# Attention over rows: one ScalarE operation copies all transposed probabilities; bias, relu and second expansion moved in the order of work

## The chip, the core and the metric

The program runs on one core of one Trainium2 chip. The time is that of the device for one execution of the whole program, in microseconds (us). Five engines have queues of their own, each worked off in order: TensorE (PE), VectorE (DVE), ScalarE (ACT), GpSimd (POOL) and SyncE (SP); semaphores tie them together.

## The reference

Eight batches of 128 tokens of width 256 pass through four pairs of attention and feed-forward. The second pair is the one that the change touches:

```python
x = x + _L1_xattn_ref(_layernorm(x), ctx, ...)   # 16 heads of 16; q, k rms-normalised over 256
x = x + _L1_ffn_ref(_layernorm(x), ...)          # 4-bit fake quantisation, 256 -> 1024 -> 256
# _L1_xattn_ref
q = rms_norm(x @ Wq + bq, gq); k_img = rms_norm(ctx_img @ Wk_img + bk_img, gk_img)
v_img = ctx_img @ Wv_img + bv_img
out = _attend(q, k_img, v_img) @ Wo + bo         # the text half is zero: the context is short
# _L1_ffn_ref
h = x_q @ W1_q.T + b1_q;  h_q = fake_quant(relu(h), s2, 0, 15)
out = h_q @ W2_q.T + b2_q
```

## The kernel before

The program works through stages 0 to 8 in one block; stages 2 and 3 (this pair) run together in `s23_pe`, `s23_act`, `s23_dve` and `s23_pool`, and their last feed-forward steps are woven into stage 4 (`s47_pe` and its fellows). The order of work on each engine is written out by hand in a loop over windows w from -4 to 15, with k = w // 2: two windows, even and odd, for each batch k. A half h = 2n + c is one group of eight heads of batch n. In window w TensorE does

- `scores(w+1)` (L1376) and `turn_probs(w)` (L1383: transposes of eight heads' probabilities into two banks of PSUM, the same two that held the scores);
- in an even window `output(k-1)` (L1406, projection of the attention), `down(k-3)` (L1442, second product of the feed-forward), then the projections of batch k+2 (L1340, L1346);
- in an odd window `turn_rows(k)` (L1419) and `turn(k+2)` (L1361, transposes of normalised queries and keys);
- `up(k-2, 0 or 1)` (L1434, first product of the feed-forward, in halves of 512 columns) and `weigh(w)` (L1398, probabilities by values, with row sums).

VectorE does `maxima(w+1)` (L1590) and its half of the copies of the transposed probabilities, `copy_probs(w)` (L1597, the second bank, 128x512). In an even window follow `add(k-1)` and `feed(k-3)` (residuals with the moments of the layernorm; L1620, L1637, L1640), `apply` (L134, the layernorm itself), `bias(k+2)` (L1564) and `values(k+2)` (L1571). In an odd window it does `normalise(k+2)` (L1581) ahead of the copy, `divide(w-1)` (L1603, L1607), and after the copy `quantise(k-2, 0)`, `divide(w)`, `quantise(k-2, 1)` (L1626, L1630).

ScalarE copies the first bank (L1485), takes the exponentials (`exps`, L1493), in an even window the sums of squares of batch k+2 (`squares`, L1504, which wait for `bias`) and then `relu(k-2, 0)` (L1527); in an odd window `copy_rows` (L1518), `copy_qk` (L1512) and `relu(k-2, 1)`. GpSimd turns the sums into inverse roots (L1686, L1689; for the layernorms L139), adds the output bias (L1702), builds the diagonal of keys (L1696) after `copy_qk`, and quantises the rows for `up` (L1706 to L1712). `c_PT` and `c_PTv` count the two copies, `c_o` counts finished `divide`s, `c_x` finished `add`s.

Who waits for what: `weigh(w)` for both copies; `divide(w)` for `weigh(w)`; `turn` for `normalise`, which waits for the roots of the squares; `up(n, 0)` for the first operation of `feed(n-1)` (they share a bank); `up(n, 1)` for `relu(n, 0)`; `quantise(n, i)` for `relu(n, i)`; `down(n)` for `quantise(n, 1)`.

Of the kernel before, what the change touches and what calls it, by code (L numbers as in the profile page):

```python
# [26 lines left out]
ACT = mybir.ActivationFunctionType  # L27
AX = mybir.AxisListType

B, T, D = 8, 128, 256  # L30
# [41 lines left out]
def build(nc, x, ctx, ctxT, mask, maskT, kvmask, a_wqT, a_wkT, a_wvT, a_bq, a_bk, a_bv, a_sel,  # L72
# [5 lines left out]
    with ex:  # L78
# [6 lines left out]
        P = ex.enter_context(nc.psum_tensor("P", [128, 8, 512], F32))  # L85
# [1144 lines left out]
        HALVES = 2 * B  # L1230
# [100 lines left out]
        def s23_pe(pe):  # L1331
# [32 lines left out]
            def scores(h):  # L1364
                n, c = divmod(h, 2)
                pe.wait_ge(c_qkT, n + 1)
                pe.wait_ge(c_kbd, h + 1)
                if h == 1:
                    pe.wait_ge(c_qkT, 2)
                    pe.wait_ge(c_v, 2)  # L1370
                if h >= 2:
                    pe.wait_ge(c_PT, h - 1)
                    pe.wait_ge(c_PTv, h - 1)
                for i in range(2):
                    half = slice(64 * i, 64 * i + 64)
                    t = pe.matmul(P[:, 2 + 2 * c + i, :], c_qT[n % 2][half, c, :], c_kb[n % 2][half, c], start=True,  # L1376
                                  stop=True)
                t.then_inc(c_s, 1)
# [8 lines left out]
            def weigh(h):  # L1387
                n, c = divmod(h, 2)
                pe.wait_ge(c_PT, h + 1)
                pe.wait_ge(c_PTv, h + 1)  # L1390
                pe.wait_ge(c_v, n + 1)
                if c == 0 and n > 0:
                    pe.wait_ge(c_x, n)
                for what in range(2):
                    for i in range(2):
                        for r in range(4):
                            j = 2 * r + i
                            t = pe.matmul(P[32 * r:32 * r + 32, 6, c * D + what * T:c * D + what * T + T],  # L1398
                                          c_one[:, i, :] if what else c_vp[n % 3][:, 8 * c + j, :],
                                          c_pt[h % 2][:, j, :], start=(i == 0), stop=(i == 1))  # L1400
                t.then_inc(c_pv, 1)
# [47 lines left out]
            for w in WINDOWS:  # L1449
                k, odd = divmod(w, 2)  # L1450
                if 0 <= w + 1 < HALVES:
                    scores(w + 1)
                if 0 <= w < HALVES:
                    turn_probs(w)
                if not odd:
                    if 0 <= k - 1 < B:
                        output(k - 1)
                    if 0 <= k - 3 < B:
                        down(k - 3)
                    if 2 <= k + 2 < B:  # L1460
                        project_context(k + 2)
                        project_rows(k + 2)
                    elif k == -2:
                        project_rows(0)
                else:
                    if 0 <= k - 1 < B:
                        turn_rows(k, 1)
                    if 0 <= k + 2 < B:
                        turn(k + 2)
                    if k == -2:  # L1470
                        project_rows(1)
                if 0 <= k - 2 < B:
                    up(k - 2, odd)
                if 0 <= w < HALVES:
                    weigh(w)
                if 1 <= w + 5 < B:
                    turn_routed(w + 5)
            return output, turn_rows, up, down

        def s23_act(act):  # L1480
            def copy_probs(h):
                act.wait_ge(c_t, h + 1)
                if h >= 2:
                    act.wait_ge(c_pv, h - 1)
                act.activation(c_pt[h % 2][:, 0:4, :].rearrange("p j t -> p (j t)"), P[:, 2 + 2 * (h % 2), :],  # L1485
                               ACT.Copy).then_inc(c_PT, 1)

            def exps(h):
                act.wait_ge(c_mx, h + 1)
# [17 lines left out]
            def copy_qk(n):  # L1507
                act.wait_ge(c_tr, n + 1)
                if n >= 2:
                    act.wait_ge(c_s, 2 * n - 2)  # L1510
                    act.wait_ge(c_kbd, 2 * n - 2)
                act.activation(c_qT[n % 2].rearrange("p j t -> p (j t)"), P[:, QK_BANK[n], :], ACT.Copy).then_inc(c_qkT, 1)  # L1512
# [25 lines left out]
            for w in WINDOWS:  # L1538
                k, odd = divmod(w, 2)
                if 0 <= w < HALVES:  # L1540
                    copy_probs(w)
                if 0 <= w + 1 < HALVES:
                    exps(w + 1)
                if not odd:
                    if 0 <= k + 2 < B:
                        squares(k + 2)
                else:
                    if 0 <= k - 1 < B:
                        copy_rows(k, 1)
                    if 0 <= k + 2 < B:  # L1550
                        copy_qk(k + 2)
                if 0 <= k - 2 < B:
                    relu(k - 2, odd)
                if 1 <= w + 5 < B:
                    copy_routed(w + 5)
            return copy_rows, relu

        def s23_dve(dve):
# [26 lines left out]
            def maxima(h):  # L1585
                dve.wait_ge(c_s, h + 1)
                if h >= 2:
# [1 line left out]
                bank = 2 + 2 * (h % 2)  # L1589
                dve.tensor_reduce(c_m[h % 2], P[:, bank:bank + 2, :].rearrange("p a (j t) -> p (a j) t", t=T), AX.X,  # L1590
                                  ALU.max, negate=True).then_inc(c_mx, 1)

            def copy_probs(h):
                dve.wait_ge(c_t, h + 1)
                if h >= 2:
                    dve.wait_ge(c_pv, h - 1)
                dve.tensor_copy(c_pt[h % 2][:, 4:8, :].rearrange("p j t -> p (j t)"),  # L1597
                                P[:, 3 + 2 * (h % 2), :]).then_inc(c_PTv, 1)

            def divide(h):  # L1600
                n, c = divmod(h, 2)
# [46 lines left out]
            for w in WINDOWS:  # L1648
                k, odd = divmod(w, 2)
                if 0 <= w + 1 < HALVES:  # L1650
                    maxima(w + 1)
                if odd and 0 <= k + 2 < B:
                    normalise(k + 2)
                if odd and 0 <= w - 1 < HALVES:
                    divide(w - 1)
                if 0 <= w < HALVES:
                    copy_probs(w)
                if not odd:
                    if 0 <= k - 1 < B:
                        add(k - 1)  # L1660
                    if 0 <= k - 3 < B:
                        feed(k - 3)
                    if 0 <= k - 1 < B:
                        apply("attend", k - 1)
                    if 0 <= k - 3 < B:
                        apply("feed", k - 3)
                    if 0 <= k + 2 < B:
                        bias(k + 2)
                        values(k + 2)
                else:  # L1670
                    if 0 <= k - 2 < B:
                        quantise(k - 2, 0)
                    if 0 <= w < HALVES:
                        divide(w)
                    if 0 <= k - 2 < B:
                        quantise(k - 2, 1)
                if 2 <= w + 6 < B:
                    routed_row(dve, w + 6)
# [1474 lines left out]
```

## Time and profile before

| | |
|---|---|
| median of 3 runs | 1213.58 us (1206.4 to 1214.52) |
| profiled execution | 1215.49 us, span 1213.5 us |
| mean granted TensorE clock | 0.947 of full |
| stages 2 and 3 with `weigh` | about 437 to 563 us of the span |

A span is the time from the first to the last instruction; the time of a run has some 2 us around it. Positions below are microseconds from the start of the span.

### The profile page before, as it was taken

To read this page: it belongs to the slowest core of one execution; us is meant where nothing else is said; L and a number is where in the kernel's file an instruction comes from. 1 tells how busy PE (TensorE), PEld (TensorE's weight loads), DVE (VectorE), ACT (ScalarE), POOL (GpSimd) and SP (SyncE) were. 2 spreads that over 40 slices of the span, in tenths; PEclk is the share of its full clock that TensorE was granted. 3 is DMA by queue.
4 is the path that set the end of the run, shared out by engine and by line. 5 is a ranking of instruction groups with operands and counts; after the bars stand their busy time and mean duration, and the time that the engine had idled before them with its cause. 6 is when DMAs were issued, how large, how long until landed. Compare 5 with 4: busy or idle time off the path is not lost.

```text
span 1213.5 us, 20040 instructions
## 1 busy us (share of the span) xinstructions
PE 1058.6 (87%) x6826; PEld 803.0 (66%) x6826; DVE 717.7 (59%) x1700; ACT 502.6 (41%) x1785; POOL 319.9 (26%) x440
## 2 busy tenths in 40 slices
PE   6898788699999868878999999999789999996694
PEld 3665555489999745656878777776556666664472
DVE  5576775711222276887656565566677777775544
ACT  2255557233333144665433334243445555554120
POOL 6252331112332233553100000001212222220572
PEclk9899999689999968989999999999999999999797
DMA  6764442689888406100111101122000000000795
GB/s 194 268 209 143 142 133 81 240 314 331 317 329 321 141 26 227 52 1 31 36 55 36 36 1 36 35 88 88 1 1 5 5 5 6 6 5 13 223 312 180
DMA packets 85218, 141.72 MB, mean 117 GB/s; under 512 B 10090, under 2 KB 58490, under 8 KB 79202
## 3 DMA queue, kind: packets, MB, share of 16 engines
q1 hardware_dynamic: 71193, 116.84, 29.1%
q0 software_dynamic: 4416, 12.06, 2.9%
q10 hardware_dynamic: 9508, 11.55, 2.8%
q8 instruction: 55, 0.90, 0.3%
q14 instruction: 46, 0.37, 0.1%
HBM read 117.51 MB, written 22.72 MB: 116 GB/s over the span
## 4 chain that ended last, share of the span: by engine, by line
PE 60%; DVE 12%; DMA 9%; issue 7%; ACT 4%; SPq 4%; POOL 3%; DVEq 0%; POOLq 0%; ACTq 0%
PE P L968 6%; PE P L978 6%; PE P L1928 4%; PE P L1968 4%; PE P L2114 4%; PE P L2061 4%; DMA scr_qk<-big 3%; PE P L1919 3%; PE P L2880 2%; PE P L2067 2%; PE P L2103 2%; PE P L2089 2%; DMA big<-placed 2%; PE P L2897 1%; PE P L1940 1%
## 5 line engine op out<-in xcount | busy, mean ns | idle before, releaser
L139 POOL TENSOR_TENSOR lrs<-lve,mhalf 128x1 f32<-128x1 f32 x64 | 36.6, 572 | 328.3 <-DVE lve L130 284.2
L576 DVE TENSOR_REDUCE small<-P 128x2 f32<-128x512 f32 x128 | 84.2, 683 | 44.4 <-PE P L403 44.4
L1009 ACT ACTIVATE big<-P,big 128x128 f32<-128x128 f32 x184 | 52.4, 368 | 124.5 <-PE P L968 124.5
L2255 ACT ACTIVATE big<-P,small 128x128 f32<-128x128 f32 x128 | 45.2, 366 | 128.4 <-DVE small L2438 128.4
L656 ACT ACTIVATE big<-P 128x512 f32<-128x512 f32 x128 | 73.6, 599 | 59.0 <-PE P L423 52.0
L968 PE MATMUL P<-big 128*128 128x128 f32 x736 | 87.5, 278 | 0.6 <-DMA big<-b_w 0.5
L968 PEld LDWEIGHTS P<-big 128*128 128x128 f32 x736 | 85.6, 195 | 1.1 <-DMA big<-b_w 1.1
L1111 DVE COPY big<-P 128x256 f32<-128x256 f32 x23 | 9.8, 425 | 125.9 <-PE P L978 125.9
L978 PE MATMUL P<-big 128*128 128x256 f32 x368 | 83.1, 379 | 0.0
L271 PE MATMUL P<-CT,big 128*128 128x256 f32 (+1 forms) x224 | 69.7, 441 | 5.7 <-ACT big L248 4.4
L978 PEld LDWEIGHTS P<-big 128*128 128x128 f32 x368 | 68.2, 190 | 8.4
L403 PE MATMUL P<-big 90*128 90x256 bf16 x256 | 51.1, 282 | 13.8 <-DVE small L576 12.2
L1919 PE MATMUL P<-XNT,big 128*128 128x128 f32 x512 | 62.6, 275 | 0.0
L2114 PE MATMUL P<-big 128*128 128x256 f32 x256 | 61.8, 385 | 0.4 <-DVE big L2635 0.4
L2356 ACT ACTIVATE big<-P 128x512 f32<-128x512 f32 x32 | 19.1, 597 | 102.5 <-PE P L2067 102.5
L2061 PE MATMUL P<-big,XNT 128*128 128x512 f32 x128 | 60.4, 594 | 1.1 <-DVE big L2579 1.1
L1968 PE MATMUL P<-big 128*128 128x256 f32 x256 | 60.6, 380 | 0.0
L1928 PE MATMUL P<-big,CT 128*128 128x512 f32 x128 | 60.1, 592 | 0.0
L1919 PEld LDWEIGHTS P<-XNT,big 128*128 128x128 f32 x512 | 59.7, 192 | 0.2 <-issue 0.2
L2347 ACT ACTIVATE big<-P,small 128x128 f32<-128x128 f32 x128 | 56.7, 459 | 5.2 <-DVE small L2624 5.2
L2429 DVE COPY big<-P 128x512 f32<-128x512 f32 x32 | 22.1, 691 | 60.5 <-PE P L1928 60.4
L1152 POOL DMA_INDIRECT moe_y<-big x23 | 25.0, 1089 | 122.3 <-DVE big L1111 122.3
(387 smaller groups left out, 2530.8 us busy)
## 6 DMA issues: line engine op xcount, KB each, us to landing
big<-b_w SPq DMA_DIRECT2D x23, 1028.0 KB
big<-b_w SPq DMA_DIRECT2D x23, 1024.0 KB
big<-scr_qk SPq DMA_DIRECT2D x96, 96.0 KB
big<-keys_t SPq DMA_DIRECT2D x8, 1024.0 KB, 6.4
big<-i_wgu SPq DMA_DIRECT2D x23, 352.0 KB
keys_t<-XNT ACTq DMA_DIRECT2D x24, 256.0 KB, 2.1
big<-moe_y SPq DMA_DIRECT2D x16, 256.0 KB, 4.3
big<-i_wd SPq DMA_DIRECT2D x23, 176.0 KB
```

What stands on the lines that cost most here:

```text
L271: t = pe.matmul(P[:, key_bank(p), lo:hi], k_wts[:, g, k, 128 * j:128 * j + 128], CT[:, k, 512 * r + lo:512 * r + hi], start=(k == 0), stop ...
L576: dve.tensor_reduce(negM[:, h, :], P[:, h % 2, :].rearrange("p (c s) -> p c s", c=2), AX.X, ALU.max, negate=True).then_inc(a_max, 1)
L656: act.activation(ER[:, g % 8], P[:, second_bank(i), :].rearrange("p (c t) -> p c t", c=2), ACT.Exp).then_inc(a_e, 1)
L968: m = pe.matmul(P[:, 2 * (j % 2) + f // 4, f % 4 * 128:f % 4 * 128 + 128], w1x[j % 3][:, k * F0 + f * 128:k * F0 + f * 128 + 128], xgT[j % ...
L978: m = pe.matmul(P[:, 6 + j % 2, 0:D], hT[j % 2][:, f, :], w2x[j % 3][:, f, :], start=(f == 0), stop=(f == FC - 1))
L1009: act.activation(hT[j % 2][:, f, :], P[:, 2 * (j % 2) + f // 4, f % 4 * 128:f % 4 * 128 + 128], ACT.Gelu_apprx_tanh, bias=w1x[j % 3][:, 2 ...
L1919: t = pe.matmul(P[:, 0, j * T:j * T + T], e_wqs[:, g, k, j * 128:j * 128 + 128], XNT[:, k, b * T:b * T + T], start=(k == 0), stop=(k == KD ...
L1928: t = pe.matmul(P[:, 2, :], CT[:, k, b * T:b * T + T], e_wvs[:, g, k, :], start=(k == 0), stop=(k == KD - 1))
L1968: t = pe.matmul(P[:, 7, 0:D], e_o[:, j, :], e_wos[:, 4 * g + j, :], start=(g == 0 and j == 0), stop=(g == 3 and j == 3))
L2061: t = pe.matmul(P[:, 0, :], XNT[:, k, b * T:b * T + T], h_wqs[:, g, k, :], start=(k == 0), stop=(k == KD - 1))
L2114: t = pe.matmul(P[:, 7, 0:D], h_o[:, j, :], h_wos[:, 4 * g + j, :], start=(g == 0 and j == 0), stop=(g == 3 and j == 3))
L2347: t = act.activation(h_pr[m % 2][:, j, :], P[:, 4 - 2 * (m % 2), j * T:j * T + T], ACT.Exp, bias=h_bi[m % 2][:, j:j + 1], scale=h_rq[:, m ...
```

## The change

In `s23` alone. ScalarE copies both banks in one operation of 128x1024 and VectorE's copy goes, with its semaphore; `weigh(h)` gets a wait for `divide(h-1)` in its place. Three steps change their place in a queue: on TensorE `up(k-2, 1)` goes ahead of `turn(k+2)`; on ScalarE `relu(k-2, 0)` goes ahead of `squares(k+2)`, and `copy_qk` ahead of `copy_rows`; on VectorE `bias(k+2)` goes ahead of both `apply`.

```diff
@@ scores, weigh (PE)
                 if h >= 2:
                     pe.wait_ge(c_PT, h - 1)
-                    pe.wait_ge(c_PTv, h - 1)
...
                 pe.wait_ge(c_PT, h + 1)
-                pe.wait_ge(c_PTv, h + 1)
+                if h > 0:
+                    pe.wait_ge(c_o, h)
@@ order of PE, odd window
                         turn_rows(k, 1)
+                    if 0 <= k - 2 < B:
+                        up(k - 2, 1)
                     if 0 <= k + 2 < B:
                         turn(k + 2)
...
-                if 0 <= k - 2 < B:
-                    up(k - 2, odd)
+                if not odd and 0 <= k - 2 < B:
+                    up(k - 2, 0)
@@ copy_probs (ACT)
-                act.activation(c_pt[h % 2][:, 0:4, :].rearrange("p j t -> p (j t)"), P[:, 2 + 2 * (h % 2), :],
-                               ACT.Copy).then_inc(c_PT, 1)
+                bank = 2 + 2 * (h % 2)
+                act.activation(c_pt[h % 2].rearrange("p j t -> p (j t)"),
+                               P[:, bank:bank + 2, :].rearrange("p a n -> p (a n)"), ACT.Copy).then_inc(c_PT, 1)
@@ order of ACT
                 if not odd:
+                    if 0 <= k - 2 < B:
+                        relu(k - 2, 0)
                     if 0 <= k + 2 < B:
                         squares(k + 2)
                 else:
+                    if 0 <= k + 2 < B:
+                        copy_qk(k + 2)
                     if 0 <= k - 1 < B:
                         copy_rows(k, 1)
-                    if 0 <= k + 2 < B:
-                        copy_qk(k + 2)
-                if 0 <= k - 2 < B:
-                    relu(k - 2, odd)
+                    if 0 <= k - 2 < B:
+                        relu(k - 2, 1)
@@ order of DVE (the function copy_probs of DVE is removed)
-                if 0 <= w < HALVES:
-                    copy_probs(w)
...
                     if 0 <= k - 3 < B:
                         feed(k - 3)
+                    if 0 <= k + 2 < B:
+                        bias(k + 2)
                     if 0 <= k - 1 < B:
                         apply("attend", k - 1)
                     if 0 <= k - 3 < B:
                         apply("feed", k - 3)
                     if 0 <= k + 2 < B:
-                        bias(k + 2)
                         values(k + 2)
```

## Rows read from the trace of the kernel before

**Rows 1.** The page, busy time of each engine, its share of the span, instructions.

```profile
PE 1058.6 (87%) x6826; PEld 803.0 (66%) x6826; DVE 717.7 (59%) x1700; ACT 502.6 (41%) x1785; POOL 319.9 (26%) x440
```

**Rows 2.** Busy time by stretch: batches 3, 4 and 5, then stage 4.

```profile
489.10:504.40 15.30, 12.60 (x140) 9.55 (x141) 13.52 (x29) 9.99 (x35) 7.98 (x10) 1.00 0.10 26
504.40:519.70 15.30, 12.55 (x136) 9.43 (x136) 13.53 (x29) 9.98 (x35) 7.97 (x10) 0.98 0.01 3
519.70:535.70 16.00, 13.89 (x136) 10.36 (x136) 13.46 (x29) 10.05 (x35) 7.98 (x10) 0.91 0.01 2
...
562.00:640.00 78.00, 75.88 (x545) 63.89 (x545) 48.66 (x119) 30.91 (x116) 9.02 (x12) 1.00 0.16 47
```

Columns: stretch, its length, then busy us and instructions of PE, PEld, DVE, ACT and POOL, the granted clock, the DMA share and GB/s.

**Rows 3.** Timeline of batch 4, from one odd `weigh` to the next.

```profile
504.37 1.08 PE L1398 MATMUL P<-big 128*32 128x128 f32 x32 [0.73 <-issue]
...
504.80 1.62 ACT L1527 ACTIVATE big<-P,small 128x128 f32<-128x128 f32 x4
...
506.71 0.71 DVE L1626 TENSOR_SCALAR big<-big 128x512 f32<-128x512 f32 x1
...
507.24 1.20 POOL L1706 TENSOR_SCALAR big<-XNT,small 128x256 f32<-128x256 f32 x1
...
507.45 0.58 DVE L1630 TENSOR_SCALAR big<-big 128x512 bf16<-128x512 f32 x1
...
509.09 0.67 DVE L1597 COPY big<-P 128x512 f32<-128x512 f32 x1
...
510.84 1.03 PE L1346 MATMUL P<-big,XNT 128*128 128x256 f32 x4
...
511.70 0.61 PE L1434 MATMUL P<-big 128*128 128x128 bf16 x8
...
513.79 0.68 DVE L1564 TENSOR_TENSOR big<-P,big 128x512 f32<-128x512 f32 x1
514.31 0.86 PEld L1383 LDWEIGHTS P<-idf,big 128*128 128x128 f32 x8 [0.76 <-issue]
...
514.51 0.42 ACT L1504 ACTIVATE big<-big 128x256 f32<-128x256 f32 x1 [3.13 <-DVE big L1564]
...
515.32 1.48 ACT L1527 ACTIVATE big<-P,small 128x128 f32<-128x128 f32 x4
...
516.51 1.33 DVE L1581 SCALAR_TENSOR_TENSOR big<-big,small 128x256 f32<-128x256 f32 x2 [0.51 <-POOL small L1689]
...
517.77 0.94 DVE L1603 RECIPROCAL big<-P 128x128 f32<-128x128 f32 x1
...
517.90 0.66 PE L1361 MATMUL P<-idf,big 128*128 128x128 f32 x4 [2.06 <-DVE big L1581]
...
518.95 0.68 DVE L1597 COPY big<-P 128x512 f32<-128x512 f32 x1
...
519.74 1.94 PE L1398 MATMUL P<-big 128*32 128x128 f32 x32 [0.73 <-issue]
```

Columns: start, length, engine, line, operation, out<-in, count, and in brackets the idle time before it with what ended it.

**Rows 4.** Groups by line, 437 to 562 us, ScalarE.

```profile
L1485 ACT ACTIVATE big<-P 128x512 f32<-128x512 f32 x16 | 9.6, 598 | 25.2 <-PE P L1383 25.2
```

Columns after the bar: busy us, mean ns of one, idle us before them and its end.

**Rows 5.** Timeline of other batches: `weigh` or `up` and their waits.

```profile
458.12 1.93 PE L1398 MATMUL P<-big 128*32 128x128 f32 x32 [1.18 <-issue]
...
474.47 1.68 PE L1398 MATMUL P<-big 128*32 128x128 f32 x32 [1.18 <-issue]
...
484.25 1.48 ACT L1527 ACTIVATE big<-P,small 128x128 f32<-128x128 f32 x4
...
542.88 0.88 PE L1434 MATMUL P<-big 128*128 128x128 bf16 x8 [2.25 <-DVE big L1637]
...
561.91 1.08 PE L1398 MATMUL P<-big 128*32 128x128 f32 x32 [0.71 <-issue]
```

**Rows 6.** Busy time by stretch, two of those at a low clock.

```profile
456.00:465.00 9.00, 7.54 (x53) 5.06 (x54) 6.07 (x12) 2.90 (x10) 2.27 (x4) 0.62 0.01 2
...
519.00:523.00 4.00, 3.27 (x37) 2.02 (x36) 2.63 (x7) 2.78 (x9) 2.44 (x3) 0.57 0.00 0
```

More of the change, by code:

```diff
@@ L1591, in maxima @@
                                   ALU.max, negate=True).then_inc(c_mx, 1)
[L1593 to L1598, printed above, removed]
             def divide(h):
```

## The prediction

> **What bounds the kernel now.** I read the page first, then busy time by stretch, then the timeline of the two stages. The page gives TensorE 87% of the span and VectorE 59% [rows 1]; that says nothing about the stage that changes. By stretch it turns round: in batches 3 and 4 VectorE is busy 13.5 us of 15.3, TensorE 12.6, ScalarE 10.0 [rows 2]; in stage 4 behind them TensorE is busy 75.9 us of 78 [rows 2], so what the two stages save should arrive at the end whole: stage 4 is limited by TensorE's own work and only starts earlier. Its loads are no limit either (DMA share 0.16 there [rows 2]).
>
> The timeline of batch 4 [rows 3] then shows the ring. I take one batch from the start of its predecessor's odd `weigh` to its own: 504.37 to 519.74, 15.37 us. TensorE stands idle twice in it: 2.06 us before `turn` (517.90), which waits for `normalise`, and 0.73 us before `weigh` (519.74). That second wait is put down to issue, but it ends 0.1 us after VectorE's copy (518.95 and 0.68), for which `weigh` also waits. `normalise` (516.51) waited for the roots of the squares; the squares (514.51) had waited 3.13 us for `bias` (513.79); and `bias`, whose data were there at 511.87 (510.84 and 1.03), came last in VectorE's even window, behind its copy (509.09), `add`, `feed` and both `apply`. So VectorE's queue sets the batch: two copies of 0.68 and a badly placed `bias` lie on the ring.
>
> **The change part by part, on batch 4.**
>
> Step 1, the even copy of VectorE (0.68) goes. `add` starts that much earlier, and `feed` ends near 511.95 in place of 512.62 (two steps of 0.4 `apply` lie between it and `bias` at 513.79, with a wait of 0.4 for a root).
>
> Step 2, `bias` forward: it would start at 511.95, just behind its data at 511.87, so 1.8 us earlier. What is late next is not `bias` but ScalarE, because of step 3.
>
> Step 3, `relu(2, 0)` ahead of `squares`: the relu can start when `up` ends (511.70 and 0.61, so 512.35) and takes 1.48 [rows 3]; the squares start at 513.73 (instructions of one queue overlap by 0.1 there), not 514.51. Only 0.8 of the 1.8 us arrives. Between squares and `normalise` lie 2.00 us (514.51 to 516.51), unchanged: `normalise` at 515.73. `maxima` in front of it waits for `scores`, which end at 514.4 as before, and ends at 515.66: just in time.
>
> Step 4, the odd copy (0.68) goes. `normalise` to `divide` is 1.26 (516.51 to 517.77), `divide` itself 1.18 (to 518.95) and 0.1 more to TensorE. The new wait of `weigh` for `divide(w-1)` is what ends last: 515.73 + 1.26 + 1.18 + 0.1 = 518.3, against 519.74. The wait adds nothing of its own: VectorE's copy stood behind that `divide` in the queue, so `weigh` waited for it already. Behind the waiting `weigh` stands only the next `scores`.
>
> Step 5, `up(2, 1)` ahead of `turn`: it fills 0.5 us of the idle time before `turn`, and `turn` then lies 0.5 us closer to `weigh`, with 0.6 us to spare against `divide`. Worth nothing by itself, nor does it cost, as `relu(2, 0)` is done by then (515.1).
>
> Step 6, ScalarE's copy of 1024 columns. The trace shows none. 512 columns take 598 ns [rows 4] and 256 take 420 [rows 3], so 0.70 ns a column and 0.96 us; two operations of 512 would be 1.20. I take 1.0, as it is one operation, and keep 0.95 and 1.2. It can't be below what one bank takes. In the even window it ends long before `weigh`. In the odd one `turn_probs` ends at 515.4 (514.31 and about 1.1), ScalarE has finished the squares at 514.7, and the copy is there at 516.5, 1.8 us before `weigh`. But everything behind it moves: exponentials, `copy_qk`, `copy_rows`, and last `relu(2, 1)`, which began 0.43 us after the start of `weigh` (504.80 against 504.37 a batch earlier) and ended 2.05 after it. It would end about 2.65 after it, and `quantise(k-3, 1)`, which began 2.34 after it (506.71), slips by 0.3; `down` behind it had a margin of 0.2. So a second ring through ScalarE, relu, `quantise`, `down`, projections, `up`, is as long as the first: 0.1 per batch at a copy of 1.0, 0.3 at 1.2. Batch 4 comes to 14.05 us: 1.3 saved.
>
> The Trainium skill speaks against the swap: "ScalarE: Activation LUTs", section Rules for kernel authors, sends cheap elementwise functions to VectorE. Here VectorE's copy of a bank takes 680 ns and ScalarE's 598 [rows 3, 4], and it is VectorE that is full. The same page (What ACT_TABLE_LOAD costs) gives an ACTIVATE with immediate operands as 186 ns and 0.833 ns a column, which would be an estimated 1.04 us for 1024; no row here shows that size, and the sum would be the same within 0.1.
>
> **The other batches.** Batch 3 is like 4 (15.3 us [rows 2]): 1.2. Batches 0 and 1 have no feed-forward and `bias` waits for its data; only the odd copy is on their path, before the `weigh`s at 458.12 and 474.47 [rows 5], each with a wait of 1.18 behind the copy: 0.6 each. Batch 2 has the first `relu(0, 0)`, at 484.25 behind the squares [rows 5]. Put ahead of them it delays the squares by 1.2 us, of which `maxima` hid 0.9; the rest and some slower `normalise` eat up the 0.68 of the odd copy: a loss of 0.1. Batch 5 lasted 16.0, part of it at a low clock; with that left as it was TensorE's own chain to `up` is on the path, and only 0.6 is won. In batch 6 and 7 there are no projections, and `up` waits for `feed` (2.25 us at 542.88 [rows 5]), so both copies count, the even one and the odd one: 1.3 and 1.2 (the last `weigh` is at 561.91 [rows 5]). Sum: 0.6 + 0.6 - 0.1 + 1.2 + 1.3 + 0.6 + 1.3 + 1.2 = 6.7 us.
>
> **The clock.** Four times in these batches TensorE fell from 2.4 to 1.2 GHz: in 456 to 465 (mean 0.62), in 519 to 523 (0.57) [rows 6], and, as the lengths of 1.68 for the `weigh` at 474.47 and 0.88 for the `up` at 542.88 show (1.08 and 0.61 at full clock [rows 3, 5]), there. `weigh` at 519.74 took 1.94 for 1.08. The two idle times before a fall sum to 3.4, 2.05, 2.8 and, as one, 2.25 us; before 504.37 it was 2.66 and nothing fell. After the change the sums should be 2.8 (batch 0), 1.3 (batch 1), 1.4 (batches 3 to 5) and 1.65 (batch 6, one copy less). All but the first are below anything that fell. In their own batches the falls cost an estimated 2.7, 1.6, 1.4 and 1.3 us: half of the stretch at the low clock, where TensorE was on the path. I count the two that are farthest from falling again, 1.6 and 1.4: 3.0 us.
>
> Together 9.7 us. Against its own time that is 1215.49 - 9.7 = 1205.8; against the median of 1213.58, 1.9 lower than the profiled execution, 1203.9. About 1% (12.1 us) is what a measurement of this kernel can tell from no change; its three runs already spread over 8.1 us.
>
> **The rivals.**
>
> A, the clock comes back everywhere: also the falls in batches 0 and 6, 2.7 and 1.3 more, so 13.7 in all: 1199.9. For it: the idle times shrink everywhere. Against: in batch 0 the 2.2 us before its `turn` stay.
>
> B, the clock falls as often as before, elsewhere perhaps: 6.7 us, 1206.9. For it: 2.66 us of idle time did not fell it and 2.05 did, so the idle sums alone don't decide.
>
> C, VectorE's copy was hidden after all, or something as long takes its place: the ring through ScalarE turns out longer than I count. If the copy costs 1.2, and `relu(k-2, 1)` pushes `quantise` by 1 us in batches 3 to 5, these win 0.3 each instead of 1.2: 3 us less, without the clock's share: 1210. A version of it is the lock that the skill describes: `quantise` moves towards GpSimd's L1706, and a VectorE operation held for the whole of that one (1.20) would add 0.6 to 0.9 to each of three batches. In the trace L1630 ran beside L1706 (507.45 beside 507.24 to 508.44) and took 0.58 [rows 3] where its twin takes 0.43: a slowing by 0.15, no hold. The Trainium skill, "SBUF — State Buffer", says that the loser of the shared port pair fully blocks; by this row it doesn't here.
>
> D, slower: the clock falls in places where it now doesn't. TensorE's idle time is split anew, 0.8 before `turn` and 0.6 before `weigh`, in every batch. A fall costs 1.4 us where TensorE's chain is the ring, which it now is. Four more falls, in batches 2, 3, 4 and 7, cost 5.6 and leave 1.1 of 6.7; from the fifth on the kernel is slower, and with three more of 1.4 in stage 4 it would be at 1216.7. Against: less idle time in each batch.
>
> **How the numbers follow.** Forecast (6.7 and about half of the clock's share) 0.42; A 0.22; B 0.18; C 0.13; D 0.05. The forecast alone spans 1202 to 1206. A and its spread reach 1197, C reaches 1211; for 8 in 10 I take 1197 to 1211.5. Faster by over 1% (below 1201.4): most of A and a fifth of the forecast, 0.31. Within 1%: 0.65. Slower by over 1%: 0.04, from D.
>
> **What would show it.** Odd `weigh` to odd `weigh` in batches 3 and 4 at 14.0 to 14.3 us; the copy at 0.95 to 1.05 us; squares 0.7 us earlier, directly behind `relu(k-2, 0)`; `normalise` at once behind `maxima`; TensorE idle for 0.6 to 0.8 us before `turn` and before `weigh`, with `weigh` just behind `divide`; VectorE idle in the even window instead (for `bias`' data and for `scores`). VectorE's busy time lower by 16 times 0.68, 10.9 us; ScalarE's higher by 16 times 0.4, 6.4. From the last `weigh` to the end the same 652 us. I would be wrong if stage 4 gave the gain back, if the copy were far above 1.2, or if the ring of ScalarE's relu were the longer one by more than 0.3.

## The result

The median of nine executions is 1202.14 us (1198.61 to 1208.41), before 1214.14 us over nine (1206.4 to 1217.05, and one slow execution of 1895.58 us that the ratio leaves out). The ratio is 0.991 with an interval of 0.9889 to 0.9931, so the kernel is 10.9 us faster, between 8.4 and 13.5. The profiled execution took 1198.61 us, the fastest of the nine; its span is 1196.8 us, against 1213.5.

Not all of these 16.7 us belong to the change. I cut both spans at the first and the last `weigh` of the stage:

| us | before | after | saved |
|---|---|---|---|
| start to `weigh(0)`, code unchanged | 450.55 | 446.11 | 4.44 |
| `weigh(0)` to `weigh(15)` | 111.36 | 98.58 | 12.78 |
| `weigh(15)` to the end | 651.59 | 652.11 | -0.52 |

The first line is chance between two executions of the same code (in the profiles of the experiments below `weigh(0)` starts anywhere from 444.56 to 451.57). The third says that stage 4 and all behind it only start earlier. The busy time by stretch has the change in it (columns as in [rows 2]): batches 1, 4 and 6, then 78 us of stage 4.

```profile
453.09:466.11 13.02, 11.32 (x114) 7.94 (x115) 10.31 (x21) 7.80 (x25) 5.43 (x8) 1.00 0.52 146
493.41:507.42 14.01, 12.58 (x137) 9.49 (x138) 12.26 (x27) 11.03 (x35) 7.86 (x10) 1.00 0.01 3
521.43:533.21 11.78, 9.49 (x120) 6.79 (x121) 10.32 (x22) 8.79 (x25) 7.05 (x8) 1.00 0.01 1
552.00:630.00 78.00, 75.87 (x520) 64.15 (x519) 46.65 (x117) 32.29 (x123) 6.10 (x9) 1.00 0.17 47
```

A batch of 14.01 us stands where 15.3 stood; VectorE is busy 12.3 in it, not 13.5; the clock is full in all of them, also in batches 1 and 6. The timeline of the changed kernel, batch 4, answers to [rows 3]. Lines of the file have moved by a few: L1569 is `bias`, L1530 relu, L1507 squares, L1595 maxima, L1488 the copy, L1586 normalise, L1601 divide, L1624 and L1628 the two steps of quantise; on GpSimd L1693 is the diagonal of keys (two operations) and L1699 the output bias.

```profile
493.41 1.08 PE L1398 MATMUL P<-big 128*32 128x128 f32 x32 [0.58 <-issue]
...
500.74 0.61 PE L1434 MATMUL P<-big 128*128 128x128 bf16 x8
...
501.10 0.69 DVE L1569 TENSOR_TENSOR big<-P,big 128x512 f32<-128x512 f32 x1
...
501.39 1.51 ACT L1530 ACTIVATE big<-P,small 128x128 f32<-128x128 f32 x4 [0.97 <-PE P L1434]
...
502.77 0.43 ACT L1507 ACTIVATE big<-big 128x256 f32<-128x256 f32 x1
...
503.47 1.23 DVE L1595 TENSOR_REDUCE small<-P 128x8 f32<-128x1024 f32 x1 [0.64 <-PE P L1375]
...
504.48 1.02 ACT L1488 ACTIVATE big<-P 128x1024 f32<-128x1024 f32 x1 [0.79 <-PE P L1382]
...
504.71 0.73 POOL L1699 TENSOR_TENSOR X<-X,big 128x256 f32<-128x256 f32 x1
...
504.78 1.34 DVE L1586 SCALAR_TENSOR_TENSOR big<-big,small 128x256 f32<-128x256 f32 x2
...
506.05 0.94 DVE L1601 RECIPROCAL big<-P 128x128 f32<-128x128 f32 x1
...
506.18 0.66 PE L1361 MATMUL P<-idf,big 128*128 128x128 f32 x4 [0.85 <-DVE big L1586]
...
507.42 1.08 PE L1398 MATMUL P<-big 128*32 128x128 f32 x32 [0.58 <-issue]
...
507.68 0.43 DVE L1628 TENSOR_SCALAR big<-big 128x512 bf16<-128x512 f32 x1
...
508.14 2.04 POOL L1693 TENSOR_TENSOR big<-big,small 128x512 f32<-128x512 f32 x2 [2.69 <-ACT big L1515]
...
508.41 1.60 ACT L1530 ACTIVATE big<-P,small 128x128 f32<-128x128 f32 x4
...
510.04 0.43 DVE L1624 TENSOR_SCALAR big<-big 128x512 f32<-128x512 f32 x1 [0.20 <-ACT big L1530]
```

`relu` starts as soon as `up` is done, the squares right behind it, `normalise` right behind `maxima`, `weigh` 0.1 us after `divide`. The one copy of 1024 columns takes 1.02 us. Two rows of GpSimd matter for what follows: the diagonal starts 0.03 us after the first half's `quantise` has ended (508.11), and `normalise` starts 0.07 us after GpSimd's output bias.

### The profile page after: what moved, and what is told of

It is laid out like the page before. It is cut to its first block, busy times and chain, and to the rows that moved or that the text cites. A ratio compares the mean times of both kernels' runs of the same rounds, so it can differ in the third digit from the quotient of the medians.

```text
span 1196.8 us, 19996 instructions
## 1 busy us (share of the span) xinstructions
PE 1049.0 (88%) x6826; PEld 797.5 (67%) x6826; DVE 709.2 (59%) x1684; ACT 510.2 (43%) x1785; POOL 320.1 (27%) x440
## 4 chain that ended last, share of the span: by engine, by line
PE 62%; DVE 11%; DMA 8%; issue 6%; ACT 5%; SPq 4%; POOL 3%; DVEq 0%; POOLq 0%; ACTq 0%
PE P L968 7%; PE P L978 7%; PE P L1925 4%; PE P L1965 4%; PE P L2111 4%; PE P L2058 4%; DMA scr_qk<-big 3%; PE P L1916 3%; PE P L2064 2%; PE P L2877 2%; PE P L2100 2%; PE P L2086 2%; PE P L1937 2%; SPq L329 2%; DMA big<-placed 1%
```

## The experiments

The measure is the batch, from one odd `weigh` to the next (batch 0 from `weigh(0)`), read from the timeline of each profiled execution. A ring is a closed chain of waits from engine to engine; the longest one sets the length of a batch. F marks a batch whose granted clock was below 0.95 of full. Ratios are to the kernel before, on the same chip. Line numbers differ by a few between kernels, so the text names the step.

| kernel | batch 0 | 1 | 2 | 3 | 4 | 5 | 6 | 7 | ratio (interval) |
|---|---|---|---|---|---|---|---|---|---|
| before | 7.57 | 16.35 F | 14.67 F | 15.23 | 15.37 | 15.99 F | 14.55 F | 11.63 | 1 |
| changed | 6.98 | 13.02 | 13.29 | 14.01 | 14.01 | 14.01 | 11.78 | 11.48 | 0.991 (0.9889 to 0.9931) |
| e1 copy only | 6.98 F | 14.67 F | 14.07 F | 15.06 | 15.18 | 15.19 | 12.81 | 12.52 F | 0.996 (0.9938 to 0.9981) |
| e2 orders only | 7.57 | 16.35 F | 15.32 F | 15.15 | 16.19 F | 15.16 | 13.57 F | 11.65 | 0.9987 (0.997 to 1.0005) |
| e3 bias only | 7.57 | 14.85 F | 13.09 | 14.10 | 14.25 | 14.24 | 14.60 F | 11.64 | 0.9954 (0.9932 to 0.9975) |
| e4 changed, squares first | 6.98 | 14.36 F | 12.89 | 13.87 | 13.88 | 13.87 | 12.43 | 11.48 | 0.9919 (0.9893 to 0.9945) |
| e5 e4, relu before copies | 6.98 | 14.36 F | 12.88 | 14.46 | 14.45 | 14.45 | 15.17 F | 11.04 | 0.9962 (0.9941 to 0.9982) |
| e6 e5, divide before maxima | 7.97 F | 14.18 F | 12.96 | 14.51 | 14.47 | 14.46 | 15.22 F | 12.63 F | 1.0001 (0.9988 to 1.0013) |
| e7 changed, short relu | 6.98 | 14.36 F | 13.50 | 14.01 | 14.00 | 14.00 | 11.79 | 10.84 | 0.9919 (0.9902 to 0.9935) |
| e8 copy and bias | 6.98 | 13.01 | 12.92 | 14.15 | 14.42 | 14.42 | 14.54 F | 12.54 F | 0.9931 (0.9915 to 0.9947) |
| e9 e4, short relu | 6.98 | 14.32 F | 12.87 | 13.51 | 13.86 | 13.86 | 13.98 F | 10.84 | 0.9928 (0.9896 to 0.996) |
| e10 e8, copy_qk first | 6.98 | 14.36 F | 12.87 | 13.86 | 13.87 | 13.86 | 12.42 | 12.73 F | 0.9891 (0.9852 to 0.993) |
| e11 e8, up first | 6.98 | 14.36 F | 13.16 | 14.15 | 14.42 | 14.43 | 12.97 | 11.47 | 0.9936 (0.9912 to 0.996) |
| e12 e4, last relus first | 6.98 | 14.31 F | 12.87 | 13.86 | 13.86 | 13.88 | 13.96 F | 11.04 | 0.9929 (0.9903 to 0.9954) |

**e1, the merged copy alone**: the diff's parts of `scores`, `weigh` and both `copy_probs`, every order as before.

```diff
-                act.activation(c_pt[h % 2][:, 0:4, :].rearrange("p j t -> p (j t)"), P[:, 2 + 2 * (h % 2), :],
-                               ACT.Copy).then_inc(c_PT, 1)
+                bank = 2 + 2 * (h % 2)
+                act.activation(c_pt[h % 2].rearrange("p j t -> p (j t)"),
+                               P[:, bank:bank + 2, :].rearrange("p a n -> p (a n)"), ACT.Copy).then_inc(c_PT, 1)
...
-                if 0 <= w < HALVES:
-                    copy_probs(w)
```

> The merged copy alone (both banks by ScalarE, none by VectorE, weigh waits for divide), every order of work as before. Theory 1 (the two VectorE copies are what lay on the ring, the new orders only move slack): with the even copy gone bias starts 0.67 us earlier, the squares behind it at once, and normalise is then held by maxima, not by the squares; batches 3 to 5 take 13.9 to 14.1 us, as in the changed kernel (14.01), and the ratio to before is 0.990 to 0.993. Theory 2 (bias and relu moved forward carry a share of their own): batches 3 to 5 stay at 14.5 us or more and the ratio is 0.995 or above.

Theory 1 fell: 15.1 to 15.2 us in batches 3 to 5 and a ratio of 0.996, as theory 2's numbers said. The clock is low in batches 0 to 2 and in batch 7 here. The timeline (relu 1, the first step of quantise, down) shows what took the copies' place:

```profile
500.50 1.61 ACT L1528 ACTIVATE big<-P,small 128x128 f32<-128x128 f32 x4
...
502.15 0.97 DVE L1620 TENSOR_SCALAR big<-big 128x512 f32<-128x512 f32 x1 [0.68 <-ACT big L1528]
...
503.79 1.05 PE L1442 MATMUL P<-big 128*128 128x256 bf16 x8 [0.71 <-DVE big L1624]
```

`relu(k-2, 1)` starts 1.45 us after the start of `weigh` (499.05), where it was 0.43; `down` waits 0.71. With `bias` still late, ScalarE's squares, relu 0, merged copy, exponentials and relu 1 stand in one row behind it. That isn't all of the 0.71: the step of `quantise` took 0.97 us for 0.42, beside GpSimd's diagonal (see e5 and e8).

**e2, the orders alone**: TensorE's, ScalarE's and VectorE's order as in the change, `c_PTv`, both copies and all waits as before.

```diff
+                    if 0 <= k - 2 < B:
+                        up(k - 2, 1)
                     if 0 <= k + 2 < B:
                         turn(k + 2)
...
+                    if 0 <= k - 2 < B:
+                        relu(k - 2, 0)
                     if 0 <= k + 2 < B:
                         squares(k + 2)
                 else:
+                    if 0 <= k + 2 < B:
+                        copy_qk(k + 2)
                     if 0 <= k - 1 < B:
                         copy_rows(k, 1)
-                    if 0 <= k + 2 < B:
-                        copy_qk(k + 2)
...
+                    if 0 <= k + 2 < B:
+                        bias(k + 2)
                     if 0 <= k - 1 < B:
                         apply("attend", k - 1)
```

> The three new orders alone (up ahead of turn, relu ahead of squares, bias ahead of apply, queries' copy ahead of rows' copy), VectorE still copies its bank. Theory 1: both copies stay in VectorE's queue; bias starts 1.2 us earlier, relu gives 0.5 of it back, maxima holds normalise until about 0.6 us earlier than before: batches 3 to 5 take 14.7 to 14.8 us, batches 0, 1, 6 and 7 gain nothing except at a clock that does not fall; ratio 0.995 to 1.0. Theory 2: batches 3 to 5 at 14.3 us or less, ratio 0.994 or below.

15.15 us in batches 3 and 5, above the 14.7 to 14.8 of theory 1; the ratio of 0.9987 lies within what it allowed. Together with the next run it says that the other orders take back what `bias` gives. The timeline (diagonal, then both steps of `quantise`, at the `weigh` of 502.13) shows one of them:

```profile
501.83 2.23 POOL L1701 TENSOR_TENSOR big<-big,small 128x512 f32<-128x512 f32 x2 [2.27 <-ACT big L1514]
...
501.95 1.21 DVE L1630 TENSOR_SCALAR big<-big 128x512 f32<-128x512 f32 x1
...
503.19 1.15 DVE L1634 TENSOR_SCALAR big<-big 128x512 bf16<-128x512 f32 x1
```

With `copy_qk` first the diagonal starts 0.3 us before `weigh`, and with VectorE's copy still in its queue `quantise(k-2, 0)` comes behind that: its steps take 1.21 and 1.15 us for 0.42 and 0.43.

**e3, bias alone**

```diff
                         feed(k - 3)
+                    if 0 <= k + 2 < B:
+                        bias(k + 2)
                     if 0 <= k - 1 < B:
                         apply("attend", k - 1)
...
-                        bias(k + 2)
                         values(k + 2)
```

> Only VectorE's bias goes ahead of both apply. Theory 1: squares stand ahead of relu on ScalarE and follow bias at once, so normalise is held by maxima behind values: batches 3 to 5 at 14.7 to 14.8 us, the same as with all three orders moved, so that moving relu and the queries' copy is worth nothing; ratio 0.995 to 1.0. Theory 2 (the orders work only together): batches 3 to 5 stay at 15.2 to 15.4 us, ratio 1.0.

14.1 to 14.25: a larger gain than either theory had, and nearly all that the whole change gains in batches 3 to 5, from one moved line and with VectorE's copy in place. `bias` filled the wait of the second `apply` for its root (0.44), `maxima` came 0.2 earlier, and the wait of 0.51 before `normalise` [rows 3] went: the roots are there now. `normalise` also overlaps less with GpSimd's output bias (L1703), and takes 1.01 us for 1.33 in batch 3 (1.16 in batches 4 and 5):

```profile
496.36 0.73 POOL L1703 TENSOR_TENSOR X<-X,big 128x256 f32<-128x256 f32 x1
...
496.76 1.01 DVE L1581 SCALAR_TENSOR_TENSOR big<-big,small 128x256 f32<-128x256 f32 x2
...
499.66 1.08 PE L1398 MATMUL P<-big 128*32 128x128 f32 x32 [0.73 <-issue]
```

Against this kernel the other three orders cost e2 1.05 us in batch 3 (15.15 against 14.10). 0.55 of it is there already when the even `weigh` starts, 8.42 us after the odd one and not 7.87: that is the long `quantise`, so it goes with `copy_qk` first. The rest is `normalise`, which starts another 0.18 later, when its roots are there, and takes 1.33 us for 1.01. That half fits relu ahead of the squares, but no run moves relu alone, so it's argued, not shown.

**e4, the changed kernel with the squares ahead of relu 0 again**

```diff
-                    if 0 <= k - 2 < B:
-                        relu(k - 2, 0)
                     if 0 <= k + 2 < B:
                         squares(k + 2)
+                    if 0 <= k - 2 < B:
+                        relu(k - 2, 0)
```

> The changed kernel with squares ahead of relu(k-2, 0) on ScalarE again. Theory 1 (scores, then maxima, hold normalise in any case): the squares come 1 us earlier, normalise at most 0.1 us; batches 3 to 5 at 13.9 to 14.0 us, batch 2 shorter by 0.1 to 0.2 than the 13.29 of the changed kernel; ratio to before as that of the changed kernel, 0.988 to 0.993. Rival (relu through the squares is the ring, as the prediction had it): batches 3 to 5 at 13.3 us or less.

13.87 us: near theory 1 and far from the rival; batch 2 is shorter by 0.4, more than either said. Relu ahead of the squares costs 0.14 per middle batch in the changed kernel. Where it goes shows at GpSimd's output bias and `normalise`:

```profile
503.64 0.73 POOL L1699 TENSOR_TENSOR X<-X,big 128x256 f32<-128x256 f32 x1
...
504.37 0.87 DVE L1586 SCALAR_TENSOR_TENSOR big<-big,small 128x256 f32<-128x256 f32 x2
```

In e4 `normalise` starts later after `weigh` than in the changed kernel, 11.71 us and not 11.37, but the output bias is through by then, and it takes 0.87 us and not 1.34. It starts later because relu 1 now stands further back on ScalarE and `down` waits 0.34 for what follows it. The same delay makes batch 6, which has no squares, longer by 0.65 (12.43 against 11.78). Over all batches squares first wins less than 0.2 us, apart from the low clock in batch 1.

**e5, relu 1 ahead of copy_qk and copy_rows** (on top of e4)

```diff
                 else:
+                    if 0 <= k - 2 < B:
+                        relu(k - 2, 1)
                     if 0 <= k + 2 < B:
                         copy_qk(k + 2)
...
-                    if 0 <= k - 2 < B:
-                        relu(k - 2, 1)
```

> Squares ahead of relu(k-2, 0), as in the run before, and besides relu(k-2, 1) ahead of copy_qk and copy_rows on ScalarE. Theory (a ring through ScalarE's relu, quantise and down holds the changed kernel: down waited 0.34 us and quantise 0.84 us in that run): relu ends 1.0 us earlier, the waits of quantise and down go, and the next bound is scores, maxima, normalise, divide: batches 3 to 5 at 13.2 to 13.5 us, batch 7 below 11.2; ratio to before 0.988 to 0.990. Rival (the ring goes through maxima and divide already): 13.8 us as before this edit.

Both missed, 14.45: slower than e4 by 0.6 in the middle batches (batch 7 is at 11.04, as the theory said). GpSimd is the bound that neither named.

```profile
497.22 2.23 POOL L1693 TENSOR_TENSOR big<-big,small 128x512 f32<-128x512 f32 x2 [5.74 <-ACT big L1515]
497.24 1.30 DVE L1628 TENSOR_SCALAR big<-big 128x512 bf16<-128x512 f32 x1
...
502.86 0.62 PE L1434 MATMUL P<-big 128*128 128x128 bf16 x8 [0.62 <-POOL big L1709]
```

The diagonal (L1693) starts when `copy_qk` ends, now 2.76 us after the start of `weigh` instead of 1.37; `up` waits 0.62 us for GpSimd's quantisation behind it. And VectorE's second step of `quantise`, 0.43 us alone, takes 1.30 when it starts with the diagonal: it ends at 498.54, 0.28 us after the first of the diagonal's two operations (1.04 us of the 2.23).

**e6, divide(w-1) ahead of maxima(w+1)** (on top of e5)

```diff
+                if odd and 0 <= w - 1 < HALVES:
+                    divide(w - 1)
                 if 0 <= w + 1 < HALVES:
                     maxima(w + 1)
...
-                if odd and 0 <= w - 1 < HALVES:
-                    divide(w - 1)
```

> The kernel with relu(k-2, 1) ahead of both copies, and divide(w-1) ahead of maxima(w+1) in odd windows on VectorE, where it waits for the scores. Theory: 0.1 to 0.3 us per batch less than that kernel (13.0 to 13.3 in batches 3 to 5), as the idle time of 0.5 us before maxima is filled; the exponentials start 0.4 us later without being late. Rival (exponentials or the copy of the probabilities last): no change or 0.3 us more.

No change in batches 3 to 5 (14.5), as the rival allowed: `up` waits 1.39 us for GpSimd's quantisation (0.62 in e5), and with GpSimd the bound, filling VectorE's gap is worth nothing there. The whole program is slower than e5 (1.0001 against 0.9962, and the intervals don't overlap); batches 0 and 7 are longer, each with a low clock in it, and what caused that isn't shown.

**e7, the changed kernel with a short relu 1**: one activation of 512 columns in place of four of 128, for relu 1 of rows 0 to 5 (run in batches 2 to 7); the biases of the other three blocks are left out by it.

```diff
-                for f in range(4):
-                    t = act.activation(d_hf[:, 4 * i + f, :], P[:, FEED_BANK[n], f * T:f * T + T], ACT.Relu,
+                for f in range(4 if i == 0 or n > 5 else 1):
+                    m = 1 if i == 0 or n > 5 else 4
+                    t = act.activation(d_hf[:, 4 * i + f:4 * i + f + m, :].rearrange("p f t -> p (f t)"),
+                                       P[:, FEED_BANK[n], f * T:(f + m) * T], ACT.Relu,
```

> The changed kernel, but relu(n, 1) of batches 0 to 5 is one operation over 512 columns in place of four of 128: it leaves out the biases of three of the four groups. ScalarE has 0.9 us less in front of quantise. Theory (the second ring is as long as the first, and sets the last batches): batches 3 to 5 shorter by 0.0 to 0.1 us (14.01 to 13.9), batch 7 shorter by 0.5 to 0.9 us (11.48 to 10.6 to 11.0). Rival (batch 7 is held by VectorE or TensorE): batch 7 at 11.4 to 11.5.

Batch 7 goes from 11.48 to 10.84, batches 3 to 5 are at 14.00: the theory in both places (batch 2 is 0.2 longer, which it didn't foresee). ScalarE in front of `quantise` sets batch 7, as the changed kernel's timeline shows:

```profile
535.16 1.59 ACT L1530 ACTIVATE big<-P,small 128x128 f32<-128x128 f32 x4
...
536.78 0.43 DVE L1624 TENSOR_SCALAR big<-big 128x512 f32<-128x512 f32 x1 [1.14 <-ACT big L1530]
...
537.82 1.05 PE L1442 MATMUL P<-big 128*128 128x256 bf16 x8 [0.58 <-DVE big L1628]
```

In the middle batches of the changed kernel `down` has no such wait, so an earlier `quantise` has nothing to give. And in e7 it doesn't end earlier either. It starts 0.28 us sooner, 2.34 after `weigh`, but beside the diagonal, and takes 0.70 for 0.43:

```profile
496.24 2.04 POOL L1695 TENSOR_TENSOR big<-big,small 128x512 f32<-128x512 f32 x2 [2.68 <-ACT big L1515]
...
497.87 0.70 DVE L1626 TENSOR_SCALAR big<-big 128x512 f32<-128x512 f32 x1
```

**e8, merged copy and bias**: the diffs of e1 and e3 together, every other order as before.

> The merged copy and bias ahead of apply, nothing else moved. Theory (of the four orders only that of bias pays; the merged copy alone left batches 3 to 5 at 15.1 us because the late bias pushed squares, relu and the copy back on ScalarE): 13.8 to 14.0 us in batches 3 to 5, ratio to before 0.989 to 0.993, as the changed kernel. Rival (up ahead of turn or the queries' copy ahead of the rows' is needed): 14.3 us or more.

14.42 us in batches 4 and 5 (14.15 in batch 3): the rival. The orders of ScalarE or TensorE do carry something, 0.55 per batch against e4.

**e10, e8 and copy_qk ahead of copy_rows; e11, e8 and up ahead of turn**: first e10's edit, then e11's.

```diff
-                    if 0 <= k - 1 < B:
-                        copy_rows(k, 1)
                     if 0 <= k + 2 < B:
                         copy_qk(k + 2)
+                    if 0 <= k - 1 < B:
+                        copy_rows(k, 1)
```

```diff
+                    if 0 <= k - 2 < B:
+                        up(k - 2, 1)
                     if 0 <= k + 2 < B:
                         turn(k + 2)
...
-                if 0 <= k - 2 < B:
-                    up(k - 2, odd)
+                if not odd and 0 <= k - 2 < B:
+                    up(k - 2, 0)
```

> Merged copy, bias ahead of apply, and copy_qk ahead of copy_rows on ScalarE; relu, squares, up and turn as in the kernel before. Theory (in the run without this third edit quantise stood beside the second operation of GpSimd's diagonal and took 0.97 us for 0.42, until that one ended; copy_qk first starts the diagonal 0.5 us earlier and takes it out of quantise's way): quantise(k-3, 1) back at 0.43 us, batches 3 to 5 at 13.8 to 13.95 us for 14.42. Rival (that quantise waits for relu anyway and the hold is hidden): 14.3 to 14.45.

> Merged copy, bias ahead of apply, and up(k-2, 1) ahead of turn on TensorE; ScalarE's orders as in the kernel before. Theory (that order only moves slack: relu(k-2, 1) stands behind the exponentials and copies on ScalarE in any case): 14.3 to 14.45 us in batches 3 to 5, as without it. Rival (an earlier up lets relu and down come earlier): 14.1 or less.

13.87 and 14.42: it is `copy_qk`. First e8, then e10, each the diagonal, the first step of `quantise`, and `down`:

```profile
513.58 2.04 POOL L1689 TENSOR_TENSOR big<-big,small 128x512 f32<-128x512 f32 x2 [4.07 <-ACT big L1513]
...
514.93 0.97 DVE L1620 TENSOR_SCALAR big<-big 128x512 f32<-128x512 f32 x1 [0.84 <-ACT big L1528]
...
516.58 1.05 PE L1442 MATMUL P<-big 128*128 128x256 bf16 x8 [0.88 <-DVE big L1624]
```

```profile
498.78 2.04 POOL L1689 TENSOR_TENSOR big<-big,small 128x512 f32<-128x512 f32 x2 [3.54 <-ACT big L1513]
...
500.68 0.43 DVE L1620 TENSOR_SCALAR big<-big 128x512 f32<-128x512 f32 x1 [0.83 <-ACT big L1528]
...
501.77 1.05 PE L1442 MATMUL P<-big 128*128 128x256 bf16 x8 [0.32 <-DVE big L1624]
```

In e8 the diagonal ends at 515.62, and `quantise`, which started at 514.93, only at 515.90; in e10 the diagonal ends at 500.82, the step starts at 500.68 and is not held. The difference in the batch is 0.55, the hold was 0.54. Batch 3 agrees: there the step took 0.97 in e8 and 0.70 in e10, and the batches differ by 0.29. "Up first" changes nothing in batches 3 to 5. E11's last two batches are shorter than e8's, but e8's had a low clock, so it isn't shown that the order does it.

**e9, squares first and short relu 1**: the diffs of e4 and e7 together.

> Squares ahead of relu(k-2, 0) and the single short relu(n, 1) together (it leaves out the biases of three of four groups in batches 0 to 5). Each alone gave batches 3 to 5 of 13.87 and 14.00 us. Theory (two rings of equal length, one through relu 0, squares and normalise, one through relu 1, quantise and down): both edits together cut what neither cuts alone, 13.3 to 13.5 us in batches 3 to 5, batch 7 at 10.6 to 10.9. Rival (a third ring, TensorE's own work or GpSimd, is just as long): 13.8 to 13.9 us.

13.86 in batches 4 and 5, the rival (batch 3, at 13.51, is where the theory put it; there only the second step of `quantise` was held, and `down` started 0.36 sooner). In batch 4 `quantise` started 2.52 us after the start of `weigh` instead of 3.27 in e4, and took 1.16 us for 0.43:

```profile
497.95 2.04 POOL L1695 TENSOR_TENSOR big<-big,small 128x512 f32<-128x512 f32 x2 [3.54 <-ACT big L1515]
...
499.12 1.16 DVE L1626 TENSOR_SCALAR big<-big 128x512 f32<-128x512 f32 x1
...
500.95 1.05 PE L1442 MATMUL P<-big 128*128 128x256 bf16 x8 [0.32 <-DVE big L1630]
```

It ran until 500.28, 0.3 behind the end of the diagonal at 499.99, and `down` waited 0.32 as in e10. So a third ring, `copy_qk`, diagonal, `quantise`, `down`, holds e9. In e4 and e10, as long at 13.87, `quantise` starts only 0.14 us before the diagonal ends, after a wait of 0.83 for relu: there the ring through relu 1 is the one that holds, and the two are equally long. No run takes the diagonal away, so what would come behind both stays open.

**e12, e4 with relu 1 ahead of copy_rows in batches 6 and 7**

```diff
+                    if k >= 6:
+                        relu(k - 2, 1)
                     if 0 <= k - 1 < B:
                         copy_rows(k, 1)
-                    if 0 <= k - 2 < B:
+                    if 0 <= k - 2 < 4:
                         relu(k - 2, 1)
```

> All edits of the change except that squares stay ahead of relu(k-2, 0); and in the last two batches, which have no copy_qk, relu(k-2, 1) goes ahead of copy_rows. Theory: batch 7 from 11.48 to 11.0 us, the others as with squares first (12.9 in batch 2, 13.87 in 3 to 5); from weigh 0 to weigh 15 98.0 us without a fall of the clock, 0.5 less than the changed kernel; ratio to before 0.989 to 0.992. Rival (GpSimd's quantise, which follows copy_rows, is then late and up waits for it): batch 7 no shorter, stage 4 starts later.

Batch 7 is at 11.04 as expected; batch 6 had a low clock and cost 1.5 us more than e4's, so the 98.0 us from `weigh(0)` to `weigh(15)` weren't reached (100.76). Its ratio can't be told from that of the changed kernel, nor can e10's, the best measured one (four executions, 0.9891), which needs three of the five edits.

## Why the prediction was right

The forecast was 1203.9 us, the median is 1202.14, and the ratio's 10.9 us stand beside my 9.7. The walk along batch 4 holds up to the last of its steps, the second ring. That the total is so close is luck in part: batch 7 was counted 1.05 us too high, and more of the clock came back than I had counted.

- **The middle batches** (steps 1 to 6 on batch 4). Forecast 14.05, measured 14.01. After the start of `weigh` the squares come at 9.36 us (forecast 9.36) and `normalise` at 11.37 (11.36); `divide` is last before `weigh`, and the idle times before `turn` and `weigh` are 0.85 and 0.58 (0.8 and 0.6). The copy took 1.02 us, forecast 1.0.
- **Whose gain it is** was wrong in the text. I said that two copies and a badly placed `bias` lie on the ring, and counted the copies as 0.68 each. In batches 3 and 4 `bias` alone gives 1.1 us (e3) and the copies alone 0.2 (e1). It is otherwise where a batch has no projections or no feed-forward: in batch 0 the copy alone gives 0.59 and `bias` nothing. Over the whole program neither can be told from the other (0.996 for e1, 0.9954 for e3), and the change with both is faster than either.
- **What holds `normalise`** I had only as the squares and `maxima`, and its own length as given. Beside GpSimd's output bias it takes 1.33 or 1.34 us (before and changed), behind it 0.87 (e4).
- **Step 3**, relu first gives away a part of `bias`: right in sign with the merged copy, and small (e4, 0.14 in a middle batch, given back in batch 6). Its cost without the merged copy isn't shown, since e2 moved `copy_qk` too.
- **Step 5**, up first is worth nothing: e11 agrees in batches 3 to 5.
- **Step 6**, a second ring through relu 1 about as long as the first, for which I added 0.1 per batch. `quantise` started 0.28 later, as forecast (0.3), but both of its steps were done 3.66 us after `weigh` as before, and `down` has no wait. The slip cost nothing because in the kernel before the first step had been held for just as long: it took 0.71 us at 506.71 and 0.42 at 519.55 [rows 3]. Shortening relu gave nothing there (e7).
- **Batches 0 to 2**: 0.59 for 0.6; 3.33 for 0.6 and a fall of 2.7; 1.38 for -0.1 and a fall of 1.6.
- **Batches 5 and 6**: 1.98 for 0.6 and 1.4; 2.77 for 1.3 and 1.3.
- **Batch 7** is the term that was mis-sized: 1.2 forecast, 0.15 measured. I had carried both copies over from batch 6 and left out the second ring, which without projections behind it shows in full: relu waits behind the merged copy and eight exponentials, and `down` waits 0.58 for it. E7 gives 0.64 of the missing 1.05 back; the other 0.4 isn't traced to a step.
- **The clock.** In the profiled execution all four falls are gone (rival A, 13.7; measured 12.78, the rest is batch 7). That is one execution, and the fastest; in the median the result lies between forecast and A. Batch 1 fell in 11 of 12 experiments' profiles (all but e8's), and in e4 with the same 2.21 and 0.58 us of idle time as in the changed kernel, which didn't fall. So the order in the queues doesn't settle it; a fall of batch 1 costs 1.34 us (14.36 against 13.02). Batch 2's and batch 5's falls, the two that I counted, are gone in every kernel that has both the merged copy and the early `bias`. Batch 6 fell in five of those nine experiments, and batch 7, which hadn't fallen before, in three: a little of rival D.
- **Rival C's lock** I dismissed by one row: L1630 beside L1706 took 0.58, not the whole 1.20 [rows 3]. That row held, but for another pair of operations than the one that mattered, and the pair that mattered stood in the same rows. L1626 at 506.71, with its 0.71 us, ran beside the diagonal, which ended at 507.14, 0.28 us before L1626 did:

```profile
505.10 2.04 POOL L1696 TENSOR_TENSOR big<-big,small 128x512 f32<-128x512 f32 x2 [3.29 <-ACT big L1512]
...
506.71 0.71 DVE L1626 TENSOR_SCALAR big<-big 128x512 f32<-128x512 f32 x1
```

Beside the diagonal, a product of two tensors, VectorE's step is held until the GpSimd operation under way ends: 0.97, 1.16 and 1.30 us for 0.43 in e8, e9 and e5. The Trainium skill, "SBUF — State Buffer", section Who interferes with whom, says that the second of the two to issue fully blocks until the other's instruction ends; these rows agree. The pair of L1630 and L1706 doesn't: VectorE's step was through 0.41 us before GpSimd's. My sum wasn't hurt, because the change keeps the two apart. With `copy_qk` first the diagonal ends 0.1 us after `quantise(k-3, 1)` begins, and with VectorE's copy gone `quantise(k-2, 0)` ends 0.03 us before the diagonal starts. In e2, which has the first and not the second, both of its steps are held.

## What to carry to other kernels

When engines feed each other in a ring, walk the new ring in order of time and take its length. Counting each removed instruction at its own length gives the wrong owner: two copies of 0.68 us were worth 0.2 in a middle batch, one moved line 1.1. Do the walk once more for the first and last turns of the loop, where other work is missing that hid a wait: there the owner can be the other one. Edits can also need each other: `copy_qk` first pays 0.55 us with the merged copy (e10 against e8), and without it sends `quantise` into the diagonal (e2). So look at which VectorE steps start while GpSimd is inside a two-tensor operation, and where the same step has two lengths in one trace, ask what ran beside the longer one.

## What was not expected of the hardware

A VectorE `tensor_scalar` of 128x512 took 0.42 us alone. When it started inside a GpSimd `tensor_tensor` of two SBUF inputs it took up to 1.30 us: in 55 of the 56 such pairs that the traces of this stage show it ended 0.27 to 0.30 us after the GpSimd operation, wherever in it it had started, and in the last, started 0.05 before that end, 0.37 after it. Beside a GpSimd `tensor_scalar` of 128x256 it took 0.41 to 0.65 us and was never held for the whole of it; there, too, GpSimd's operation shows in where it ends (started 0.1 or 0.2 us into L1703, it took 0.65 or 0.58 and ended 0.4 before L1703 did in the changed kernel). Falls of TensorE's clock differ between executions of kernels with the same idle times: batch 6 fell in e12 and not in e4, with the same orders up to there.
